# The routing stage of a mixture-of-experts kernel: early products of the shared network moved to GpSimd, half-tile slots, down weights in quarters

## What is computed

```python
x = x + rwkv(_layernorm(x), ...)          # time mixing
x = x + ffn(_layernorm(x), ...)           # first MoE layer
x = x + retention(_layernorm(x), ...)
x = x + ffn(_layernorm(x), ...)           # second MoE layer

def ffn(x, router_w, router_bias, wg, wu, wd, swg, swu, swd):   # E, F, K = 64, 64, 4
    logits = flat @ router_w                                     # flat: 4096 x 256
    scores = softmax(logits)
    _, topk_idx = top_k(logits + router_bias, K)
    topk_scores = take_along_axis(scores, topk_idx); topk_scores /= topk_scores.sum(-1)
    comb = zeros((n, E)).at[arange(n)[:, None], topk_idx].set(topk_scores)
    g = silu(einsum('nd,edf->nef', flat, wg)); u = einsum('nd,edf->nef', flat, wu)
    routed = einsum('ne,nef,efd->nd', comb, g * u, wd)
    sg = silu(einsum('nd,sdh->nsh', flat, swg)); su = einsum('nd,sdh->nsh', flat, swu)
    shared = einsum('nsh,shd->nd', sg * su, swd)                 # the shared network, 2 x 256 wide
    return routed + shared
```

## Time and profile before

| | |
|---|---|
| three timed executions | 2129.87, 2136.06, 2137.48 us |
| the profiled execution | 2127.3 us, span 2125.6 us |
| TensorE matmul / VectorE / ScalarE / GpSimd busy | 1541.5 / 1082.2 / 520.2 / 892.1 us |
| mean granted TensorE clock | 0.798 |
| route, first layer | 232 to 594 us |
| route, second layer | about 1355 to 1717 us |
| w_gu / w_d by layer | 8192 KB / 4096 KB |

### The profile page before, as it was taken

How to read it: one execution, slowest core, us unless ns; L and a number is a source line. 1 busy time by engine, 2 the same in 40 slices (tenths; PEclk the granted TensorE clock), 3 DMA queues, 4 the chain that set the end, 5 groups by cost and what they waited for, 6 DMA issues and landing times. The chain is left out here.

```text
span 2125.6 us, 27096 instructions
## 1 busy us (share of the span) xinstructions
PE 1541.5 (73%) x7272; PEld 1051.1 (49%) x7273; DVE 1082.2 (51%) x2619; ACT 520.2 (24%) x973; POOL 892.1 (42%) x885
## 2 busy tenths in 40 slices
PE   6565579633978988837898889479824978888850
PEld 3333455321657766624555556455411567666630
DVE  6665579300144554424857576588400235444538
ACT  5666241000122222213132121241000122222210
POOL 4666335775035555531010101134776025555540
PEclk9787559855988888768898899659955988888875
DMA  9500001622164444325334310001633065444419
GB/s 368 213 1 0 34 0 48 256 105 91 34 163 146 143 141 138 93 71 180 121 121 174 123 63 1 34 0 38 240 116 105 16 163 148 135 136 134 122 56 344
DMA packets 132857, 245.22 MB, mean 115 GB/s; under 512 B 24434, under 2 KB 94118, under 8 KB 132276
## 3 DMA queue, kind: packets, MB, share of 16 engines
q1 hardware_dynamic: 101524, 176.74, 26.7%
q0 software_dynamic: 30720, 67.74, 8.6%
q10 hardware_dynamic: 544, 0.00, 0.0%
HBM read 121.38 MB, written 139.74 MB: 123 GB/s over the span
## 5 line engine op out<-in xcount | busy, mean ns | idle before, releaser
L1009 POOL DMA_INDIRECT pairs_y<-arena x384 | 380.4, 991 | 456.7 <-DVE arena L1109 330.4
L777 POOL DMA_INDIRECT slots_x<-arena x256 | 268.4, 1048 | 81.2 <-issue 79.2
L1042 PE MATMUL moe_eh<-arena 128*128 128x128 f32 x1536 | 248.5, 314 | 63.9 <-DVE arena L1101 60.3
L1042 PEld LDWEIGHTS moe_eh<-arena 128*128 128x128 f32 x1536 | 226.4, 226 | 74.1 <-ACT arena L1073 70.9
L1053 PE MATMUL moe_ey<-arena 64*128 x768 | 248.3, 449 | 1.3 <-DVE arena L1122 1.3
L1114 DVE TENSOR_TENSOR arena<-arena,moe_eh 64x256 f32<-64x256 f32 x192 | 81.2, 423 | 304.9 <-PE moe_ey L1053 184.3
L630 PE MATMUL moe_gate<-arena 128*128 (+1 forms) x256 | 138.9, 661 | 81.4 <-issue 43.9
L1073 ACT ACTIVATE arena<-moe_ext 128x512 f32<-128x512 f32 x192 | 114.6, 597 | 252.6 <-PE moe_ext L1031 131.5
L643 PE MATMUL moe_tp<-arena 128*128 128x256 f32 x512 | 124.4, 403 | 69.4 <-issue 66.8
L1053 PEld LDWEIGHTS moe_ey<-arena 64*128 64x128 f32 x768 | 146.9, 212 | 45.4 <-issue 13.0
L1031 PE MATMUL moe_ext<-ident,arena 128*128 128x128 f32 x768 | 141.0, 312 | 29.5 <-DMA arena<-slots_x 23.0
(11 more groups left out here) (208 smaller groups left out, 2290.2 us busy)
## 6 DMA issues: line engine op xcount, KB each, us to landing
slots_x<-empty_slots SPq DMA_DIRECT2D x96, 520.0 KB, 8.8
arena<-slots_x SPq DMA_DIRECT2D x192, 260.0 KB
arena<-pairs_y SPq DMA_DIRECT2D x64, 512.0 KB
arena<-w_gu SPq DMA_DIRECT2D x2, 8192.0 KB
pairs_y<-arena POOLq DMA_INDIRECT x384
residual<-x SPq DMA_DIRECT2D x8, 512.0 KB
slots_x<-arena POOLq DMA_INDIRECT x256
out<-residual SPq DMA_DIRECT2D x4, 1024.0 KB, 9.3
```

Of the source, the lines that this page charges most:

```text
L777: pool.indirect_dma_start(out=slots.x, in_=xn[:, t, :], in_offset=None, out_offset=bass.IndirectOffsetOnAxis(ap=slot[:, t, i:i + 1], axis=0))\
L1009: pool.indirect_dma_start(out=slots.y, in_=ytile[:, n % YRING, j, :], in_offset=None, bounds_check=slots.pairs - 1, oob_is_err=False, out_ ...
L1042: last = pe.matmul(h_ps[place % 2][:, j * P:(j + 1) * P], weights[:, place % 2, j, h, :], xt[:, place % 2, (j * KH + h) * P:(j * KH + h + ...
```

## The change

It touches the route alone, so it acts twice.

- Blocks 0 and 1 of the shared network: ScalarE copies the up bank to a new SBUF tile `su` behind each silu, and GpSimd multiplies (`multiply_early`, 8 products) ahead of its scatter. VectorE multiplies blocks 2 to 7.
- The chain's steps from the start of an expert to the positions are made for 16 of the 32 tiles first; the slots of choice 0 for these are announced on their own, and the other half follows after `add_down(0)` and `add_down(1)`.
- All products up to block 7 are put between the steps of the chain and of the gates. `dispatched` now comes after `multiply(7, 3)`.
- TensorE makes gate_up(n+1, 0), gate_up(n+1, 1), down(n), gate_up(n+1, 2), gate_up(n+1, 3). `multiply(n, 0)` waits until down(n-1) is complete.
- The loops of the route are unrolled on all engines, and `xst` is gone: the router reads `xnt`.
- The scatter's semaphores go by quarters of 8 tiles. The down weights of experts 33 to 63 are loaded after the last gate_up in one piece, those of 0 to 32 in four, each when its quarter has been scattered.

```diff
-            sp.wait_ge(sem("scattered0"), 16 * K * NT // 2)
-            load_down(0, WD_HALF)
-
-            sp.wait_ge(sem("gu_full"), SH * (NB - 1))
-            load_down(WD_XNT, WD_LAST)
-
+            WD_QUARTER = [q * QUARTER * W // D for q in range(4)]
             sp.wait_ge(sem("gu_full"), SH * NB)
-            load_down(WD_LAST, E)
-
-            sp.wait_ge(sem("scattered1"), 16 * K * NT // 2)
-            load_down(WD_HALF, WD_XNT)
+            load_down(WD_XNT, E)
+            for q in range(3):
+                sp.wait_ge(sem(f"scattered{q}"), 16 * K * QUARTER)
+                load_down(WD_QUARTER[q], WD_QUARTER[q + 1])
+
+            sp.wait_ge(sem("scattered3"), 16 * K * QUARTER)
+            load_down(WD_QUARTER[3], WD_XNT)
...
             def gate_up(n, j):
-
-                pe.wait_ge(sem("sht_ready"), SH * n + j + 1)
+                g = SH * n + j
+                if 2 <= g < EARLY + 2:
+                    pe.wait_ge(sem("su_ready"), g - 1)
+                elif g >= EARLY + 2:
+                    pe.wait_ge(sem("sht_ready"), g - 1)
...
-            for j in range(2):
-                gate_up(0, j)
+            gate_up(0, 0)
+            gate_up(0, 1)
             rank(NB - 1)
-            for j in range(2, SH):
-                gate_up(0, j)
-            down(0)
-            with pe.Fori(1, NB) as n:
-                for j in range(SH):
-                    gate_up(n, j)
+            gate_up(0, 2)
+            gate_up(0, 3)
+            for n in range(NB - 1):
+                gate_up(n + 1, 0)
+                gate_up(n + 1, 1)
                 down(n)
+                gate_up(n + 1, 2)
+                gate_up(n + 1, 3)
+            down(NB - 1)
...
+            def keep_up(j):
+                act.activation(su[:, j % 2, :], up_ps[j % 2][:, :], ACT.Copy).then_inc(sem("su_ready"), 1)
...
+            def multiply_early(n, j):
+                pool.wait_ge(sem("su_ready"), SH * n + j + 1)
+                if n and j == 0:
+                    pool.wait_ge(sem("down_full"), 2 * n)
+                pool.tensor_tensor(sht[:, j, :], sg[:, j % 2, :], su[:, j % 2, :], ALU.mult)\
+                    .then_inc(sem("sht_ready"), 1)
+
+            for n in range(EARLY // SH):
+                for j in range(SH):
+                    multiply_early(n, j)
             HALF = NT // 2
             for i in range(K):
-                pool.wait_ge(sem("slots_ready"), i + 1)
                 for half in range(2):
+                    pool.wait_ge(sem("slots_ready"), 2 * i + half + 1)
                     if i:
 
-                        pool.wait_ge(sem(f"scattered{half}"), 16 * HALF * i)
+                        for q in range(2 * half, 2 * half + 2):
+                            pool.wait_ge(sem(f"scattered{q}"), 16 * QUARTER * i)
...
             def multiply(n, j):
                 dve.wait_ge(sem("sg_ready"), SH * n + j + 1)
+                if j == 0:
+                    dve.wait_ge(sem("down_full"), 2 * n)
...
+            start_less_count(FRONT)
+            start_on_base(FRONT)
+            positions(FRONT)
+            pick(0, FRONT, pos)
+            slot_of(0, FRONT)
+            dve.sem_inc(sem("slots_ready"), 1)
+            add_down(0)
+            start_less_count(BACK)
+            start_on_base(BACK)
+            positions(BACK)
+            add_down(1)
+            multiply(2, 0)
+            multiply(2, 1)
+            pick(0, BACK, pos)
+            slot_of(0, BACK)
+            dve.sem_inc(sem("slots_ready"), 1)
+            multiply(2, 2)
+            pick(1, ALL, pos)
+            multiply(2, 3)
+            slot_of(1, ALL)
+            dve.sem_inc(sem("slots_ready"), 2)
+            pick(2, ALL, pos)
+            add_down(2)
+            multiply(3, 0)
...
             c.link(dve.tensor_reduce(gate_sum, gate, AX_X, ALU.add))
             c.link(dve.reciprocal(gate_sum, gate_sum))
-            multiply(3, 3)
+            multiply(7, 2)
+            multiply(7, 3)
             c.link(dve.tensor_tensor(gate, gate, gate_sum.unsqueeze(2).to_broadcast([P, NT, K]), ALU.mult))
             dve.sem_inc(sem("dispatched"), 1)
-            add_down(3)
-            with dve.Fori(4, NB) as n:
-                for j in range(SH):
-                    multiply(n, j)
-                add_down(n)
+            add_down(7)
```

More of the change, by code:

```diff
@@ L520, in experts @@
     xs = arena.take(2, BLK, D)
-    xst_at = arena.at
-    xst = arena.take(KH, N)
+    sg = arena.take(2, N)
+    su_at = arena.at
     biased = arena.take(BLK, E)
@@ L528, in experts @@
     assert SH <= 2 * BLK * D // N
-    sg = arena.take(2, N, at=xst_at)
     sht = arena.take(SH, N, at=xs_at)
+    su = arena.take(2, N, at=su_at)
+    EARLY = 2 * SH
+    QUARTER = NT // 4
     arena.at = at_experts
@@ L611, in score @@
                     for h in range(KH):
-                        last = pe.matmul(lg[:, j, :], xst[:, h, j * P:(j + 1) * P], rw[:, h, :],
+                        last = pe.matmul(lg[:, j, :], xnt[:, h, N * n + j * P:N * n + (j + 1) * P], rw[:, h, :],
                                          start=h == 0, stop=h == KH - 1)
@@ L625, in gate_up @@
             def gate_up(n, j):
-                pe.wait_ge(sem("sht_ready"), SH * n + j + 1)
+                g = SH * n + j
[3 more added lines that the diff above has]
+                    pe.wait_ge(sem("sht_ready"), g - 1)
                 for bank, at in ((gate_ps[j % 2], j * P), (up_ps[j % 2], (SH + j) * P)):
                     for h in range(KH):
-                        last = pe.matmul(bank[:, :], sgu[:, h, at:at + P], xnt[:, h, bass.ds(N * n, N)],
+                        last = pe.matmul(bank[:, :], sgu[:, h, at:at + P], xnt[:, h, N * n:N * (n + 1)],
                                          start=h == 0, stop=h == KH - 1)
@@ L697, in keep_counts @@
                     .then_inc(sem("counts_read"), 1)
-            transposed(0, 0, is_first=True)
+            transposed(0, 0)
             transposed(1, 1)
             exp(0)
-            with act.Fori(1, NB // 2) as g:
-                for place in range(2):
-                    n = 2 * g + place
-                    transposed(n, place)
-                    exp(n - 1)
-                    keep_counts(n - 2)
+            for n in range(2, NB):
+                transposed(n, n % 2)
+                exp(n - 1)
+                keep_counts(n - 2)
             exp(NB - 1)
@@ L722, in _ @@
                 silu(0, j)
-            with act.Fori(1, NB) as n:
+                keep_up(j)
+            for j in range(SH):
+                silu(1, j)
+                keep_up(j)
+            for n in range(2, NB):
                 for j in range(SH):
@@ L749, in _ @@
             power(1, 1)
-            with pool.Fori(0, NB // 2 - 1) as g:
-                for place in range(2):
-                    power(2 * g + place + 2, place)
-                    add_choices(2 * g + place)
+            for n in range(NB - 2):
+                power(n + 2, n % 2)
+                add_choices(n)
             add_choices(NB - 2)
@@ L861, in _ @@
             choose(1)
-            with dve.Fori(1, NB // 2 - 1) as g:
-                for place in range(2):
-                    n = 2 * g + place
-                    normalise(n + 1, 1 - place)
-                    statistics(n + 2, place)
-                    choose(n)
+            for n in range(2, NB - 2):
+                normalise(n + 1, 1 - n % 2)
+                statistics(n + 2, n % 2)
+                choose(n)
             normalise(NB - 1, 1)
@@ L870, in _ @@
             choose(NB - 1)
-            dve.wait_ge(sem("xn_kept"), NB)
-            multiply(0, 0)
-            multiply(0, 1)
             dve.wait_ge(sem("counts_read"), 2 + 2 * NB)
@@ new lines, in pick, with slot_of, gate_of @@
+            def pick(i, part, of):
+                c.link(dve.tensor_tensor(picked[:, part, :], hot[i][:, part, :], of[:, part, :], ALU.mult))
+            def slot_of(i, part):
+                c.link(dve.tensor_reduce(slot_f[:, part], picked[:, part, :], AX_X, ALU.add))
+                c.link(dve.tensor_copy(slot[:, part, i], slot_f[:, part]))
+            def gate_of(i):
+                c.link(dve.tensor_reduce(gate[:, :, i], picked, AX_X, ALU.add))
+            ALL = slice(0, NT)
+            start_less_count(FRONT)
@@ new lines, in _ @@
+            pick(1, ALL, pos)
[5 more added lines that the diff above has]
+            multiply(3, 0)
+            multiply(3, 1)
+            slot_of(2, ALL)
+            dve.sem_inc(sem("slots_ready"), 2)
+            multiply(3, 2)
+            pick(3, ALL, pos)
+            multiply(3, 3)
+            slot_of(3, ALL)
+            dve.sem_inc(sem("slots_ready"), 2)
+            add_down(3)
@@ L914, in _ @@
+            multiply(4, 0)
+            multiply(4, 1)
             dve.wait_ge(sem("tile_no"), 1)
```

123 lines of the change are left out of this document (59 added, 64 removed).

## The result

The changed kernel took 2216.39 us (median of four runs, 2204.62 to 2225.11); the kernel before, on the same chip, took 2132.97. The ratio is 1.0375, 95% interval 1.0337 to 1.0414: slower by 3.8%. The forecast of 2018 us was wrong; the rival R1 (2218 us) came out in its price and in its cause, except that its condition for when the late words begin stays open. The medians differ by 83 us.

A forecast was written before the change was run, and what follows sets the result against it. The route's shared network was held from 402 to 527 by late words; the expert stage moves from 593.95 to 537.5, 56.5 us a layer, 113 for two, from 2127.3: 2014 or 2023, taken as 2018; range 1988 to 2090.

The forecast's parts named there:

- R1: Rival, chance 0.13: late words come from the scatter, not w_gu; stall to 531, expert stage at 635, 2218 us in all.
- late words: In the route, word that TensorE has finished reaches other engines late, 1.40 us an instruction; the forecast blamed w_gu's load.
- the first part: The prediction's account of what bounds the kernel: the route all but stands from 402 to 527; w_gu issued at 390.38.
- (6): w_gu released at 475.1 instead of 390.4: the 136 us holding blocks 4 and 5 go; load no longer hidden early.
- (1): Route loops unrolled, one copy of each transposed tile: 2.5 us saved (bounds 0 and 4), choosing ends at 310.2.
- (2): Blocks 0 and 1 multiplied on GpSimd ahead of the scatter: costs 5.4 us (bounds 3 and 9), first scatter at 344.2.
- (3): First slots for half the tiles: there at about 328, but GpSimd is busy until 343, so this gains nothing.
- (4): The route's scatter, 128 issues as before beside seven long VectorE products: 175.7 us, end at 519.9.
- (5): TensorE's new order in the shared network: 22.0 us a block, last product ends at 474.7, down(7) at 481.
- (7): Down weights by quarters: 23.3 us of loads besides w_gu's 21 and the scatter; next stage at 537.5 (bounds 528 and 548).
- the gap: Stretch from 402 to 527 in the kernel before's route, where the stage all but stands; expected to go.

The follow-up runs named there:

- late_dispatch_again: Kernel before with one line moved: `dispatched`, which releases w_gu's load, raised behind VectorE's loop over the blocks; repeated on a chip with late words; 2205.82 us beside 2140.5.
- after_paced: Changed kernel with one waited-for GpSimd memset of 128x192 behind each routing scatter DMA (pitch 1.52 us); 2079.39 us, ratio 0.973 to the kernel before.
- sets 2 to 4: Three of five sets of follow-up runs, each on one chip, 3 and 4 on the same; the kernel before took 2154.33, 2140.5 and 2136.06 us.
- after_again: Changed kernel, unchanged, run again on another chip beside the kernel before; 2219.75 us, ratio 1.0337.
- late_start_again: Kernel before with the whole scatter held until the second gate-and-up step of block 2 is done, on a chip with late words; 2194.14 us beside 2136.06.
- bursts: Kernel before with 32 chained GpSimd memsets ahead of each of scatter choices 1 to 3, three rests of 11.75 us; 2091.47 us beside 2154.33.
- late_dispatch: Kernel before with `dispatched`, which releases w_gu's load, raised behind VectorE's loop instead of ahead of add_down(3), on a chip without late words; 1902.83 us, ratio 1.0128.
- paced_64: Kernel before with one waited-for GpSimd memset of 128x64 behind each routing scatter DMA, on a chip without late words; 1917.5 us, ratio 1.0222.
- before_again: Kernel before, unchanged, run again on the second set's chip for its trace; 2147.32 us.
- paced_192: Kernel before with one waited-for GpSimd memset of 128x192 behind each routing scatter DMA (pitch 1.52 us); 2066.94 us, ratio 0.9679.

## Why the prediction was wrong, point by point

**The step that failed** is in the first part and in (6): that w_gu's load sets off the late words. I took it from an order of events: block 3's down is 2.3 us late at 395.85, SP issues w_gu at 390.38, and 52 us of scatter before that show nothing. late_dispatch_again has the same late words with no w_gu load until 584.20. What else changed at 390 was in the same rows: VectorE's last long product is at 378.38, and with it the 3.01 us issues of the earlier trace rows go. The prediction named exactly this as R1 ("once VectorE leaves GpSimd in peace"), with the evidence for it that decides: late words for 95 us after w_gu's traffic had ended. A cause that has been gone for 95 us is a weak one; 0.13 for R1 against 0.64 was the wrong way round. One reading beside it was off: the last word comes not 9 but 10.7 us after the scatter's last packet (515.6, and 526.33).

**"The 136 us in which blocks 4 and 5 were held go"** (6): they stayed, 397.67 to 530.29 here. R1's price was right, term by term: stall to 531 (530.3), two and a half blocks of 22 us, w_gu at 586 (589.07), loads and latencies to 635 (634.22).

**(1)** was to save 2.5 us; the choosing ends 1.2 us later (the last op starts at 312.53, before at 311.30). The stalls of 0.28 us are gone, but six normalisations of a block take 2.57 us each, where five took 1.73 and one 2.10: 4.7 us, more than was saved. Their code is the same in both kernels; what changed is what runs beside them. Each is four operations, of 0.40 us when alone. With the loops unrolled, GpSimd's three products for the sums of choices follow each other at once (252.60 to 254.86), and the three of the four operations that begin while a product runs take 0.76 to 0.83 us; in the kernel before, one begins beside the product at 253.31 (0.76 us) and the others do not. The sum in (1) had left this wait out.

**(2)** was under-sized: the scatter starts at 349.13 and not at 344.2, 10.3 us later than the 338.81 of the kernel before. My upper bound was 9. Four of the 4.9 us past the forecast come from (1): TensorE's first gate product starts at 309.73, 1.6 later than in the kernel before (308.16), where I had taken 2.5 off and put it at 305.7. The products themselves were priced well (1.27 us; 2.96 at 323.33 and 3.47 for two at 339.78 beside VectorE). The Trainium skill's rule (SBUF — State Buffer, "SBUF: two separate sides") had put up to 4 us on this start; the trace agrees that products beside VectorE's ops are stretched (2.96 against 1.27), but little of the delay is theirs.

**(3)** held: the front slots are there at 335.9, later than the 328 I gave, and GpSimd is busy until 348.6; the back slots' cast is at 364.32, ahead of the copy that needs them at 371.98. The half-tile chain gains nothing.

**(4)** 175.7 us for the scatter; 168.9 from first to last issue (349.13 to 517.99). The end at 519.9 came out (518.95) by luck: the start is 4.9 us late and the scatter some 6 us shorter, as less of VectorE's work lay beside it (28.20 us busy in 338 to 390, where the earlier trace rows has 45.14).

**(5)** 22.0 us a block: 22.3 where nothing holds it (410.43 to 477.28 in after_paced is three blocks). (7) could not be seen at work in the changed kernel. In after_paced, where w_gu is issued at 482.32, the stage after starts at 565.36, some 9 us after the scatter's last issue at 556.21, in line with "the scatter ends it" and the loads of w_gu and the down weights hidden under it. The size of these loads held in the changed kernel, where nothing hides them: 589.07 to 634.22 is 45 us, against 21 + 23.3.

**With the words on time** the forecast's net gain was mostly the gap itself. Cleared by a pause, the gap is worth some 140 us in the changed kernel (2216 or 2220 without, 2073 or 2079 with it, on different chips where the kernel before took 2133 to 2154) and 69 us in the kernel before (2136 to 2067, on one chip), though the pause lengthens the scatter in both.

## What to carry to other kernels

When a stall begins near two events, look at when it ends and at which of the two still exists then: here the stall lived 95 us longer than the traffic I blamed and ended with the scatter. When a long load is released by a step at the end of an engine's program order, price it for the case that this order is late; moving one release line behind the loop cost 65 us by itself. A pause is only cheap on an engine that idles: some 0.3 us behind each scatter DMA of the route gained 3%, while a pause in a stage where GpSimd had 1.83 us for each DMA and needed 2.08 with the pause cost 76 us a layer.

## What the runs showed of the hardware

On the chips of the first pair and of sets 2 to 4, TensorE's completion words reach the other engines late, one instruction per 1.40 us, while GpSimd issues scatter DMAs at a pitch of 1.27 us beside TensorE's work. At the end of the scatter they come all together, 10 to 15 us after the start of its last issue (516.10 to 526.57 in after_again, 513.57 to 526.41 in before, 517.99 to 530.29 in after, 511.82 to 524.67 in late_dispatch_again, 533.53 to 548.10 in late_start_again). In bursts the held silu at 444.68 comes 0.5 us after the rest begins at 444.19, so this is no fixed delay. A pitch of 1.52 us shows none of it, rests of 11.75 us clear it. Where in the chip the words wait is not shown.

It depends on the chip: the same program took 1878 and 1882 us on two chips and 2133 to 2154 us on the others. The difference shows in the stages with indirect DMAs: the next stage starts at 538.42 in late_dispatch on the first set's chip and at 629.33 in the same kernel on the third set's, and the expert stage takes 289.5 us (paced_64) against 355.8 (before_again). So a tuning is worth what its chip makes of it: the pause of 128x192 gained 3% on one chip (paced_192), and even the smaller one of 128x64 lost 2% on another (paced_64). No run had the same pause on both. Whether it is the chip itself or its condition at the time is not shown either.

A normalising VectorE operation (TENSOR_SCALAR, 128x256 float32) that begins while a GpSimd product runs takes 0.76 to 0.83 us instead of 0.40 (before and after, at 252 to 255 us).
